# Turning the identity, unread, ahead of TensorE's waits in two attentions

## The reference

```
x = x + xattn0(layernorm(x), ctx)   # 16 heads of 16, 120 keys per batch, masked
x = x + moe0(layernorm(x))          # 64 experts, top 8, capacity 128, and a shared expert
x = x + xattn1(layernorm(x), ctx)   # the same shape, biases, no mask
x = x + moe1(layernorm(x))          # 32 experts, top 6 of 2 groups of 4, shared and anchor experts
```

## Time and profile before

| | us |
|---|---|
| median of 3 runs | 1102.74 |
| lowest and highest | 1100.43, 1111.35 |
| the profiled execution | 1102.11 |
| its span, first to last instruction | 1100.4 |
| attention 0, about | 20 to 283 |
| experts of layer 0, about | 283 to 485 |
| attention 1, about | 490 to 750 |
| experts of layer 1 and the end | 788 to 1100 |

### The profile page before, as it was taken

How to read it: one execution, slowest core, us unless ns; L and a number is a source line. 1 busy time by engine, 2 the same in 40 slices (tenths; PEclk the granted TensorE clock), 3 DMA queues, 4 the chain that set the end, 5 groups by cost and what they waited for, 6 DMA issues and landing times. The chain is left out here.

```text
span 1100.4 us, 23121 instructions
## 1 busy us (share of the span) xinstructions
PE 938.3 (85%) x6360; PEld 687.4 (62%) x6360; DVE 643.0 (58%) x3193; ACT 474.8 (43%) x1594; POOL 612.7 (56%) x529
## 2 busy tenths in 40 slices
PE   5988888766899999879997998858699999999980
PEld 2666656544468889557765766644587767777750
DVE  3676666444245455346866766657465656565548
ACT  2776566533123343327645454221154544444430
POOL 1015555555617777693143434546588888888861
PEclk9898888666899999989969767568899999999985
DMA  9997511001679997660011241275799998888888
GB/s 330 345 374 270 174 51 48 33 19 40 224 212 315 320 317 124 124 199 32 23 63 61 74 168 64 79 298 224 232 185 254 217 154 147 155 152 158 147 233 314
DMA packets 133712, 191.19 MB, mean 174 GB/s; under 512 B 17988, under 2 KB 111117, under 8 KB 132562
## 3 DMA queue, kind: packets, MB, share of 16 engines
q1 hardware_dynamic: 85234, 126.74, 35.5%
q0 software_dynamic: 41280, 54.57, 25.2%
q10 hardware_dynamic: 7072, 8.40, 2.3%
HBM read 101.14 MB, written 99.77 MB: 183 GB/s over the span
## 5 line engine op out<-in xcount | busy, mean ns | idle before, releaser
L988 POOL DMA_INDIRECT buf<-R,RI x240 | 234.9, 979 | 330.0 <-ACT R L1150 153.6
L1036 POOL DMA_INDIRECT yb<-YT,DI x98 | 151.4, 1545 | 64.7 <-DVE DI L1610 40.0
L773 PE MATMUL PS<-R,XT 128*128 x632 | 152.1, 364 | 0.0
L317 PE MATMUL PS<-R 128*128 128x256 f32 (+2 forms) x352 | 125.1, 490 | 13.1 <-DMA R<-in_ctxT 10.0
L1618 DVE COPY XT<-PS 128x256 f32<-128x256 f32 x222 | 93.7, 422 | 35.0 <-PE PS L322 20.3
L773 PEld LDWEIGHTS PS<-R,XT 128*128 128x128 f32 x632 | 104.6, 194 | 7.5 <-issue 0.7
L1036 POOL DMA_INDIRECT yb<-AS_,DI x62 | 95.9, 1546 | 18.9 <-issue 11.6
L317 PEld LDWEIGHTS PS<-R 128*128 128x128 f32 (+1 forms) x352 | 72.6, 226 | 48.0 <-issue 36.6
L789 PE MATMUL PS<-R,AT 128*128 (+1 forms) x316 | 101.5, 404 | 0.0
L1907 DVE TENSOR_TENSOR AC<-SL,PS 128x128 f32<-128x128 f32 (+1 forms) x158 | 43.2, 273 | 89.2 <-ACT SL L1325 59.5
L1150 ACT ACTIVATE R<-R,MX 128x120 f32<-128x120 f32 x256 | 80.0, 387 | 34.3 <-DVE MX L1440 27.3
(11 more groups left out here) (209 smaller groups left out, 1897.6 us busy)
## 6 DMA issues: line engine op xcount, KB each, us to landing
R<-in_ew SPq DMA_DIRECT2D x64, 384.0 KB
BX<-buf SPq DMA_DIRECT2D x128, 140.0 KB
yb<-Z SPq DMA_DIRECT2D x34, 512.0 KB
R<-buf SPq DMA_DIRECT2D x94, 140.0 KB
R<-in_w SPq DMA_DIRECT2D x8, 1536.0 KB, 21.5
buf<-Z SPq DMA_DIRECT2D x8, 1120.0 KB, 13.3
R<-yb SPq DMA_DIRECT2D x16, 512.0 KB, 3.5
R<-yb SPq DMA_DIRECT2D x8, 1024.0 KB, 16.9
```

The source lines that it names most:

```text
L317: m = e.matmul(out_, left, right, start=(i == 0), stop=(i == len(pairs) - 1))
L773: x = e.matmul(PS[:, 2 + j % 2, 0:2 * wd], XT[:, j % 3, k, :], src[:, bass.ds(regs[j], 1), k * 2 * wd:(k + 1) * 2 * wd].rearrange("p a n - ...
L988: e.indirect_dma_start(out=(buf1 if l else buf0)[:, :], out_offset=bass.IndirectOffsetOnAxis(ap=RI[:, n % 6, k:k + 1].bitcast(U32), axis=0 ...
L1036: e.indirect_dma_start(out=yb[:, :], out_offset=bass.IndirectOffsetOnAxis(ap=DI[:, j:j + 1].bitcast(U32), axis=0), in_=(YTS0 if i < E0 els ...
```

## The change

A helper `keep_going(m, n)` issues `n` turns of the identity against itself, 128x128 each, into a bank `m` that is about to be overwritten. Nothing reads them, and they wait for nothing and signal nothing. It stands at three places for each tile: before `values` at the tile's first unit (3 turns in attention 0, 1 in attention 1; the wait for `d_cx` moves ahead of it), before the wait for the normalised rows `d_hr` (3 turns), and before the wait for their turned copy `a_h2t` (3 turns). At the last two the bank is taken, with its own wait, before the turns; at the last, that puts the bank's wait ahead of the one for `a_h2t`. In all there are 16 x (3 + 1) + 32 x 6 = 256 turns, each a weight load and a matmul.

```
+                def keep_going(m, n):
+
+                    for i in range(n):
+                        e.transpose(m[:, P * (i % 2):P * (i % 2) + P], ident, ident)
+
...
                 def values(u):
                     n = u // 2
                     b = n // 2
+                    if u % 2 == 0:
+                        if n:
+                            w.wait_ge("d_cx", 16 * l + n)
+                        keep_going(PS[:, 6, 0:256], 3 if l == 0 else 1)
                     if l == 0:
                         w.wait_ge("a_pt", 2 * u + 2)
...
+                    m = bank("h2t", n, sem="a_h2t", n=16 * l + n + 1)
+                    keep_going(m, 3)
                     w.wait_ge("d_hr", 16 * l + n + 1)
-                    tr2(e, bank("h2t", n, sem="a_h2t", n=16 * l + n + 1), HR[:, n % 6, 0:D]).then_inc(S["s_h2t"], 1)
+                    tr2(e, m, HR[:, n % 6, 0:D]).then_inc(S["s_h2t"], 1)
                     yield from pause(3)
-                    w.wait_ge("a_h2t", 16 * l + n + 1)
                     if l == 0:
                         w.wait_ge("l_wr0", 16)
                         m = bank("rt", n, sem="d_lg", n=n + 1)
+                        keep_going(m, 3)
+                        w.wait_ge("a_h2t", 16 * l + n + 1)
...
                     else:
                         w.wait_ge("l_small", 128)
                         m = bank("rt", n, sem="a_sco", n=n + 1)
+                        keep_going(m, 3)
+                        w.wait_ge("a_h2t", 16 * l + n + 1)
```

## The result

| | before | changed |
|---|---|---|
| median of 20 runs each, us | 1108.11 | 1116.49 |
| lowest and highest | 1097.69, 1115.06 | 1109.5, 1132.19 |
| the profiled execution | 1102.11 | 1114.11 |
| its span | 1100.4 | 1112.4 |

What follows compares the result with a forecast made beforehand. TensorE was taken as the bound, its clock low in much of both attentions. From the profiled 1102.1 us, 28 given back and 15 paid made 13 us less: 1089, range 1066 to 1116.

Steps and rivals of the forecast that it cites:

- the late stretches: Attention 0: VectorE's unexplained waits of about 5.6 us for TensorE, 4 times; a longer list adds 0, at most 2 us.
- the give-back: Both attentions: turns filling lulls keep TensorE's clock high, returning 0.45 of the most that could be recovered, 28 us.
- the ceiling: Most time a full clock could return: 49 us in attention 1 and 14 in attention 0, together 63 us.
- The lull with 0.90 us of work: Before one fall of TensorE's clock, busy 0.90 of five microseconds; the fall was not expected to go.
- The price of 0.46: On TensorE in both attentions, one low-clock microsecond full of work gives back 0.46 us if it were high.
- The cost of the turns: TensorE's list: 178 of 256 turns exposed, 30 us extra; 19 reach the end, 15 with a better clock.
- The covered waits: Turns hidden by existing waits: 12 of 16 groups at values in attention 0, 13 of 64 at the normalised rows and copies.
- The moved waits: Waits for `d_cx` and the banks, placed ahead of the turns, were claimed to cost nothing.
- The falls: 18 clock falls after lulls in the attentions; those after 88 to 93 and 146 to 151 were expected to go.
- The wash: Rival, chance 0.25: in the attentions only a quarter of the recoverable time returns, 16 us, and 17 are paid: 1101.
- Slower, the turns stand in the way: Rival, chance 0.15: turns hold up TensorE's list where 51 of 64 groups find waits met; 19 us, up to 30; 1121.
- Turns don't feed the clock: Rival, chance 0.08: nothing given back, both attentions' clock as before while TensorE's busy time grows; 1121 us.

Runs made afterwards that it cites:

- e13: Kernel before with only the three waits moved as in the change, no turns, on a 1100 chip: 1099.38 us, 0.997 of the kernel before.
- e15: Kernel before with the waits moved and the 112 turns of attention 1 alone, on a 1100 chip: 1115.14 us, 1.0054 of the kernel before.
- e12: The change with twice the turns, 512 in all, on a 1100 chip: 1.0106 of the kernel before.
- e6: The kernel before, unchanged, run once for its profile on a chip where it takes 995 to 998 us; no ratio.
- e14: Kernel before with the waits moved and the 144 turns of attention 0 alone, on a 1100 chip: 1107.22 us, 1.0033 of the kernel before.
- e4: Kernel before, GpSimd waiting for earlier scatters to land ahead of a tile's first and fifth, on a 1000 chip: 1110.73 us, 1.1101 of the kernel before.
- e5: The changed kernel run again, unaltered, on a 1000 chip: 998.02 us, 1.0028 of the kernel before.
- e17: Kernel before with GpSimd's waits for landed scatters only while an attention is at work, on a 1000 chip: 1079.07 us, 1.0839 of the kernel before.
- e16: Kernel before, GpSimd waiting for earlier scatters to land ahead of a tile's first and fifth, on a 1100 chip: 1110.78 us, one execution, no ratio.

## Why the prediction was wrong, step by step

**Two steps failed: the late stretches, put at 0, and the give-back, 0.45 of the ceiling.** In place of the 0 the runs show a step of 7.8 us with such a stretch in it; in place of 28 us given back, 14 to 18 by the clock. The medians moved by +8.4 us and the traces by +12.0, where the sum had -13. The traces divide the 12.0 us so: +8.5 to the end of attention 0, +6.3 in the experts of layer 0, -4.9 in attention 1 and +2.1 after it.

**The late stretches.** I had the row that told of stretches in which VectorE waits for a signal of TensorE, could not tell what they are, and wrote "I take 0 and keep 2". I also wrote that a shift in their number would be something that I did not price. It came: 22.4 us in 4 waits at the output projection became 26.5 in 6 (80 to 330). And the one step in which attention 0 loses 7.8 us, from 98.02 to 120.47, has such a stretch, which the kernel before does not have there. The changed kernel (start, us, engine; in brackets the idle time before it and what ended it):

```profile
101.66 0.48 PE L317 MATMUL PS<-R 128*128 128x256 f32 x1
...
102.81 0.47 PE L317 MATMUL PS<-R 128*128 128x256 f32 x1 [0.66 <-issue]
103.53 0.38 PE L317 MATMUL PS<-R 128*128 128x256 f32 x1 [0.25 <-issue]
104.23 0.63 PE L317 MATMUL PS<-R 128*128 128x256 f32 x1 [0.33 <-issue]
105.65 0.59 PE L480 MATMUL PS<-C,R 128*120 128x128 f32 x2 [0.79 <-issue]
107.07 1.10 PE L480 MATMUL PS<-C,R 128*120 128x128 f32 x3 [0.83 <-issue]
108.51 0.88 PE L480 MATMUL PS<-C,R 128*120 128x128 f32 x3 [0.34 <-issue]
108.78 0.38 ACT L1130 ACTIVATE R<-PS 128x256 f32<-128x256 f32 x1 [7.56 <-remote]
```

and the same work in the kernel before:

```profile
102.25 1.13 PE L317 MATMUL PS<-R 128*128 128x256 f32 x4
103.22 1.04 PE L475 MATMUL PS<-C,R 128*120 128x128 f32 x8
```

The same twelve matmuls run from 102.25 to 104.3 there and from 101.66 to 109.4 here, with no wait shown; the clock falls within the stretch, at 104.4. The step has a mean clock of 0.77, against 0.93 before. TensorE's idle time without a wait grew by 6.6 us from 80 to 283. The kernel before has a stretch of this kind later, from 123 to 128.7, again with the fall of the clock in it:

```profile
123.20:128.70 5.50, 3.58 (x16) 0.81 0.19 70
128.70:134.00 5.30, 5.30 (x44) 0.50 0.09 30
```

The changed kernel has that one too, to 135.8. Of the 10 low stretches of attention 0 after 80 in the kernel before, six, with 68 of 92 us, begin within such a stretch or about 2 us beside it. The lull with 0.90 us of work in the earlier trace rows is one. I take it that such a lull is not filled by giving TensorE more instructions, since it is TensorE that is held up; no run tests this by itself, but in the step shown the added turns filled nothing. I had counted these low stretches into the ceiling. Why the turns bring TensorE into this one is not shown (e13 and e15 above).

**The give-back.** 0.45 of the ceilings' low microseconds would have been 86 us (0.45 of 84 and of 107). Over whole executions 39 us less were low than in the kernel before, and 30 less than with the waits moved alone; the 60 us that the windows beside e12 give (88 to 68 in attention 0, 118 to 78 in attention 1) compare different work. At 0.46 that is 14 to 18 us, not 28. The price of 0.46 itself fits TensorE's busy time: from 20 us to the last *values* of attention 0 the kernel before is busy for 195.9 us with 84 us low on the 1100 chip, and for 168.2 with 20 low on the 1000 chip (e6), 27.7 us less for 64 low ones. How much of the change's 14 to 18 us reached the end can't be read off: nothing of it shows in attention 1, which took 233.4 us from its first to its last *values*, and 238.6, 229.7 and 238.2 in before, e13 and e14, without turns there.

**The cost of the turns** was charged 19 us, 15 with a better clock, as time in line. That attention 0 lost 8.5 us, where I charged 8, is luck: 7.8 of it is the one step. An estimate of the gross cost: with a turn at 0.13 us high and 0.24 low and a clock of about 0.86, 256 turns are some 41 us of TensorE's time; its busy time grew by 22.4, so the clock gave back some 19, and idle time shrank by 10.4, so some 31 us of the turns were not covered, where I charged 15. It is worked out from one trace of each kernel, and idle time also changes with the late stretches. On 1000 chips nearly all is covered: TensorE waits there from 80 to 283 for ScalarE's H2T 8 times and 10.2 us (e6), on the 1100 chip 4 times and 2.5 us. There is less waiting for other engines to hide in where TensorE is itself late.

**The covered waits.** Those for the copies at *values* shrank by 10.5 us and those for H2T by 1.6, but 6.4 us of "issue" came in ahead of *values*. **The moved waits** were priced at 0; their ratios, 0.9969 and 0.997, would be 3 us, at the edge of what the runs can tell.

**The falls.** That after 93 went (93 to 98 is at 1.00 in the change); a new one came at 104.4, within the late stretch shown above. The mean clock of attention 1 after its first 45 us was to go from 0.71 to 0.83, and it is 0.84; that of 100 to 265 was to reach 0.88 and stayed at 0.81. The expert layer was to be unchanged; it took 6.3 us longer, but with no turn in attention 0 it is 10 us longer in e15 and 2 in e13. Its 6.3 us are therefore not shown to come from the turns.

**Small slips in the sums.** The wash has 16 back and 17 paid, which is 1103 and not 1101. The busy share of the low stretches is 0.70 from the rows named, not 0.72. The 1102.1 us that the sum starts from lay at the median of 3 executions; that of 20 is 1108.1.

**Which rival it was.** "Slower, the turns stand in the way" is nearest: its condition was less than 37 us of low clock recovered, and 30 to 39 were. Its 19 us with the clock as it is would be too much for the 8.4 measured, and its place, all groups with a wait already met, is not where attention 0 lost its time. "Turns don't feed the clock" is refuted by the whole executions, 0.873 and 0.877 without turns, 0.892 and 0.911 with them. The rule quoted from the Trainium skill, "TensorE: Matmul & The Clock Gate", Part 4, is not borne out in this case: the clock rises with the number of turns, and the same eight turns take 1.04 and 1.92 us at the two levels.

What sets a 1100 chip apart from a 1000 chip, and what holds TensorE up after scatters, is not shown. That its instructions come late is one possibility; the trace shows about as many packets on the instruction queues on either kind (21 in the kernel before and 23 in e6, from 80 to 265), and no run tests it.

## What to carry to other kernels

A low granted clock is lost time of the engine, but unread work pays only where it falls into waits for other engines' products; ask first what the engine was held up by when the clock fell, and if that is no such wait, do not count on more instructions in the same list to fill it. Before a loss is called a cost in line, compare the two traces at a milestone of each tile: a cost in line grows with the tiles, and here the loss was a single step. Take a row that you cannot explain as a bound on the whole ceiling, not as a small term of its own. Compare clocks over the same work or over whole executions, not in fixed windows. Before unread work is put into the list of the busiest engine, move the waits alone and run that: here it was the better half of the change.

## What the runs showed of the hardware

- The same kernel took 995 to 998 us on three chips and 1101 to 1108 in three other rounds, on at least two chips; attention 0 ended at 220.7 (e6) against 266.6, at the same steps of code.
- On the latter, VectorE and ScalarE waited 2 to 13 us for signals that the trace does not place, and TensorE's instructions often came 0.7 us and more apart, in stretches that end shortly after a row of GpSimd's indirect transfers (one each 1.28 us). In the kernel before each of the 8 such stretches from 80 to 300 ends 0.6 to 2.3 us after a row: a row of four to 157.9 with the stretch to 159.4 (5.2 us), eight to 127.0 with that to 128.8 (5.5), twelve to 244.8 with that to 247.1 (6.6). On the former a row of 36 (174.7 to 220.5) did nothing of the kind, and there is no such stretch in e4, e5, e6 or e17.
- With rows of at most four and about 2 us between them these waits fell on VectorE from 31.0 to 6.5 us and stayed on ScalarE (29.7 and 30.2), from 80 to 330 (e16).
- Waiting for scatters to land after every four costs GpSimd 160.9 us in 54 waits (e4), 113 us of the kernel's time on a 1000 chip (e4) and 9 on a 1100 chip (e16, one execution).
- Turns of the identity count for TensorE's clock: over whole executions on 1100 chips a mean of 0.873 and 0.877 without them, 0.892 with 256 and 0.911 with 512. Turns of 16 rows did not (0.930 against 0.934 without and 0.945 with full ones, on one 1000 chip).
